# Selective scan with a mixture of experts on one core: turned state, scaled copies and sums cut into halves of the chunk

## What is computed

```
x_one = ln(x);  u = ln(x_one)*g1 + b1
x_in, z = split(u @ in_w.T);  xc = silu(causal_conv4(x_in))          # 256 channels
dt, B, C = split(xc @ xproj_w.T);  delta = softplus(dt @ dt_w.T + b)
h[t,d,n] = exp(delta[t,d]*A[d,n]) * h[t-1,d,n] + delta[t,d]*xc[t,d]*B[t,n]   # 16 states n
y[t,d]   = sum_n h[t,d,n] * C[t,n] + xc[t,d]*D[d]
x_two = x_one + (y * silu(z)) @ out_w.T
x = x + x_two + silu(gate)*val @ ffp_w.T + ffp_b      # gate, val from ln(x_two)
out = x + sum over the top 2 of 8 experts of w_e * (silu(m@Wg_e)*(m@Wu_e)) @ Wd_e    # m = ln(x)
```

## Time and profile before

| | |
|---|---|
| median of 3 runs | 898.7 us (896.98 to 903.21) |
| the profiled execution | 898.42 us, span 896.5 us |
| mean granted TensorE clock | 0.884 |
| busy: PE / DVE | 666.5 us (74%) / 726.3 us (81%) |
| busy: ACT / POOL | 504.6 us (56%) / 573.2 us (64%) |

### The profile page before, as it was taken

The page is one execution under the profiler, slowest core; times in us unless marked ns, Lnnn a source line. Parts: engine busy times, 40 slices in busy tenths (PEclk is TensorE's granted clock), DMA queues, the critical chain, the costliest instruction groups (busy, mean ns, idle before and its releaser), DMA issues. The chain is left out here.

```text
span 896.5 us, 13066 instructions
## 1 busy us (share of the span) xinstructions
PE 666.5 (74%) x3706; PEld 481.6 (54%) x3706; DVE 726.3 (81%) x1128; ACT 504.6 (56%) x1092; POOL 573.2 (64%) x488
## 2 busy tenths in 40 slices
PE   4358578678768886797788768877884877898963
PEld 2134245445335534774477446744673556798963
DVE  1378779989998999979998999999999865474363
ACT  2547676766766576556756575557553663443421
POOL 1095556566856895789768985888669934345332
PEclk9679699889879977998799988988797889999997
DMA  6833133213312336542654255434642423457794
GB/s 179 248 113 114 47 94 118 79 65 108 119 48 90 106 100 185 152 127 86 186 162 118 90 171 155 125 106 132 173 150 80 129 63 99 135 160 216 204 311 130
DMA packets 95450, 118.24 MB, mean 132 GB/s; under 512 B 11351, under 2 KB 63395, under 8 KB 95363
## 3 DMA queue, kind: packets, MB, share of 16 engines
q1 hardware_dynamic: 90835, 108.02, 41.3%
q0 software_dynamic: 4544, 9.38, 2.9%
HBM read 105.37 MB, written 16.34 MB: 136 GB/s over the span
## 5 line engine op out<-in xcount | busy, mean ns | idle before, releaser
L695 POOL TENSOR_TENSOR inflow<-du,b_wide 128x1024 f32<-128x1024 f32 x128 | 316.2, 2473 | 170.6 <-DVE product L960 109.4
L950 DVE TENSOR_TENSOR_SCAN state<-decay,carry,inflow 128x512 f32<-128x512 f32 x192 | 235.0, 1265 | 6.2 <-ACT decay L814 5.8
L814 ACT ACTIVATE decay<-delta,a_neg 128x512 f32<-128x512 f32 x256 | 171.9, 690 | 104.6 <-DVE state L950 101.1
L722 POOL DMA_INDIRECT y_dram<-y_rows,x_rows x78 | 86.8, 1112 | 82.0 <-ACT y_rows L870 73.4
L960 DVE TENSOR_TENSOR product<-state,c_wide 128x1024 f32<-128x1024 f32 (+1 forms) x98 | 135.8, 1386 | 2.8 <-PE y L1150 1.7
L1150 PE MATMUL y<-ident,product 128*128 128x128 f32 x704 | 106.2, 297 | 41.9 <-DVE product L960 41.8
L1150 PEld LDWEIGHTS y<-ident,product 128*128 128x128 f32 x704 | 87.2, 153 | 79.9 <-DVE product L960 50.0
L1155 PE MATMUL y<-h_rows,ident 128*128 128x512 f32 x160 | 101.2, 755 | 33.6 <-ACT h_rows L779 33.6
L716 POOL DMA_INDIRECT row_dram<-m_tok,place x64 | 72.7, 1136 | 25.8 <-issue 19.8
L950 DVE TENSOR_TENSOR_SCAN state<-decay,inflow 128x512 f32<-128x512 f32 x64 | 74.8, 1212 | 9.2 <-ACT decay L814 6.6
L1106 PE MATMUL work_front<-u_t,w_tap 128*128 128x512 f32 x128 | 64.1, 628 | 6.0 <-ACT u_t L750 4.4
(11 more groups left out here) (210 smaller groups left out, 1285.1 us busy)
## 6 DMA issues: line engine op xcount, KB each, us to landing
b_wide<-bc_dram SPq DMA_DIRECT2D x128, 256.0 KB, 3.3
w_stage<-gate_up_dram SPq DMA_DIRECT2D x78, 344.0 KB
c_wide<-bc_dram SPq DMA_DIRECT2D x98, 256.0 KB, 3.5
x_rows<-row_dram SPq DMA_DIRECT2D x78, 65.0 KB, 3.6
x_tok<-in_x SPq DMA_DIRECT2D x8, 256.0 KB, 6.2
out<-x_tok SPq DMA_DIRECT2D x8, 256.0 KB, 4.6
inflow<-y_dram SPq DMA_DIRECT2D x6, 256.0 KB, 4.2
gate_up_dram<-in_Wg SPq DMA_DIRECT2D x1, 1376.0 KB, 8.9
```

What stands on the lines that cost most here:

```text
L695: e.tensor_tensor(inflow[:, key % 3], du[:, c % 2], b_wide[:, key % ROW_SLOTS:key % ROW_SLOTS + 1, :].to_broadcast([P, HALVES, CHUNK]), AL ...
L722: e.indirect_dma_start(y_dram, bass.IndirectOffsetOnAxis(x_rows[:, key % X_SLOTS, ID_AT:ROW].bitcast(u32), 0), y_rows[:, key % Y_SLOTS, :] ...
L814: e.activation(decay_bank[h][:], delta[:, c % 2, h, :], ACT.Exp, scale=a_neg[:, h, n:n + 1]).then_inc(S["decay"], 1)
L950: e.tensor_tensor_scan(state[:, key % STATE_SLOTS, h, :], decay_bank[h][:], inflow[:, key % 3, h, :], 0.0 if c % (SEQ // CHUNK) == 0 else ...
```

## The change

`total`, `h_turn` and `c_scale` are each cut into two steps, one for each half of the chunk (each half is one bank of `y_bank` and one of `h_bank`). The semaphores `y_sum` and `h_turn` count halves, and each step waits for its own half alone: `h_turn0` for the first two copies of the unit before, `c_scale0` for `h_turn0` and the first half's sum, each half of `y_gate` for its own sum. In `plan()` the sum over the second half of unit i-1 (`total1`) moves behind `scan` and `decay` if unit i is shared: in a full share unit the list has `h_turn0`, `c_scale0`, `total1` of the unit before, `h_turn1`, `c_scale1`; in a half share unit `total1`, `h_turn1`, `c_scale1`. The second part of a row of `BACK`, which holds `n_t` and `m_t`, `y_cols` and `gate_h`, now comes ahead of these steps; that of `FRONT` stays behind them. The sets of shared units are the same.

```
@@ plan() @@
         if i:
-            put("total", i - 1)
+            put("total0", i - 1)
+            if i not in shares:
+                put("total1", i - 1)
         put_all(back[0], front[0])
...
+        put_all(back[1])
         if i in shares:
-            put("h_turn", i)
-            put("c_scale", i)
-        put_all(back[1], front[1])
+            if share_of(c, n) == SUB:
+                put("h_turn0", i)
+                put("c_scale0", i)
+            put("total1", i - 1)
+            put("h_turn1", i)
+            put("c_scale1", i)
+        put_all(front[1])
@@ counts @@
-        turned = [sum(k > 0 for k in share[:i + 1]) for i in range(len(UNITS))]
+        turned = [sum(share[:i + 1]) // 2 for i in range(len(UNITS))]
@@ ScalarE @@
-                elif name == "c_scale":
+                elif name in ("c_scale0", "c_scale1"):
+                    r = int(name[-1])
                     c, n = UNITS[key]
-                    e.wait_ge(S["h_turn"], turned[key])
-                    e.wait_ge(S["y_sum"], key)
+                    e.wait_ge(S["h_turn"], turned[key] - 1 + r)
+                    e.wait_ge(S["y_sum"], 2 * key - 1 + r)
                     e.wait_ge(S["c_rows"], c + 1)
-                    for sub in range(SUB - share[key], SUB):
+                    for sub in (2 * r, 2 * r + 1):
@@ VectorE @@
                     if key >= 2:
-                        e.wait_ge(S["y_sum"], key - 1)
+                        e.wait_ge(S["y_sum"], 2 * (key - 1))
...
                 elif name == "y_gate":
-                    e.wait_ge(S["y_sum"], D_STATE * (key + 1))
...
                     for r in range(2):
+                        e.wait_ge(S["y_sum"], 2 * D_STATE * (key + 1) - 1 + r)
@@ TensorE @@
-                    alone = SUB - share[key]
-                    if alone:
+                    if 2 * r < SUB - share[key]:
                         e.wait_ge(S["times_c"], products[key])
-                    for s in range(alone):
-                        for h in range(HALVES):
...
+                        for s in (2 * r, 2 * r + 1):
+                            for h in range(HALVES):
...
-                    if share[key]:
-                        e.wait_ge(S["c_scaled"], scaled[key])
-                    for r in range(alone // 2, 2):
+                    else:
+                        e.wait_ge(S["c_scaled"], scaled[key] - 2 * (1 - r))
                         t = e.matmul(y_bank[r][:], ident[:], h_rows[:, 2 * r:2 * r + 2, :].rearrange("p s d -> p (s d)"), start=False, stop=n == D_STATE - 1,
...
-                elif name == "h_turn":
+                elif name in ("h_turn0", "h_turn1"):
+                    r = int(name[-1])
                     e.wait_ge(S["scan"], HALVES * (key + 1))
                     if scaled[key] > share[key]:
-                        e.wait_ge(S["c_scaled"], scaled[key] - share[key])
+                        e.wait_ge(S["c_scaled"], scaled[key] - share[key] - 2 * (1 - r))
```

More of the change, by code:

```diff
@@ L123, with share_of @@
 HELD_ROUND = CHUNKS - 3
+def share_of(c, n):
+    return (SHARES_LAST if c == CHUNKS - 1 else SHARES).get(n, 0)
 def plan(shares=()):
@@ L267, in plan @@
         send()
-        if not moving and ("x_turn", m) not in done and n in (SHARES_LAST if c == CHUNKS - 1 else SHARES):
+        if not moving and ("x_turn", m) not in done and share_of(c, n):
             free.append(i)
         put("times_c", i)
-    put("total", len(UNITS) - 1)
+    for r in range(2):
+        put(f"total{r}", len(UNITS) - 1)
     queue_back(CHUNKS - 1)
@@ L446, in mamba_moe_block @@
         pair_of = [0 if m < tail else (1, 0, 2)[(m - tail) % 3] for m in range(len(JOBS))]
-        share = [(SHARES_LAST if c == CHUNKS - 1 else SHARES)[n] if i in shares else 0 for i, (c, n) in enumerate(UNITS)]
+        share = [share_of(c, n) if i in shares else 0 for i, (c, n) in enumerate(UNITS)]
         products = [sum(k < SUB for k in share[:i + 1]) for i in range(len(UNITS))]
         scaled = [sum(share[:i + 1]) for i in range(len(UNITS))]
-        turned = [sum(k > 0 for k in share[:i + 1]) for i in range(len(UNITS))]
+        turned = [sum(share[:i + 1]) // 2 for i in range(len(UNITS))]
         c_fetched = [sum(share[j] < SUB for j in range(i % ROW_SLOTS, i + 1, ROW_SLOTS)) for i in range(len(UNITS))]
         place_of = {step: k for k, step in enumerate(order)}
-        tiles_ahead = {i: sum(place_of["y_rows", m] < place_of["h_turn", i] for m in range(len(JOBS))) for i in shares}
-        scaled_ahead = [max((scaled[i] for i in shares if place_of["c_scale", i] < place_of["x_turn", m]), default=0) for m in range(len(JOBS))]
+        tiles_ahead = {i: sum(place_of["y_rows", m] < place_of["h_turn1", i] for m in range(len(JOBS))) for i in shares}
+        scaled_ahead = [max((scaled[i] for i in shares if place_of["c_scale1", i] < place_of["x_turn", m]), default=0) for m in range(len(JOBS))]
         held_by = [max((q for q in range(m) if pair_of[q] == pair_of[m]), default=None) for m in range(len(JOBS))]
@@ L1132, in _ @@
                     t.then_inc(S["z"], 1)
-                elif name == "total":
+                elif name in ("total0", "total1"):
+                    r = int(name[-1])
                     c, n = UNITS[key]
-                    if n == 0:
+                    if n == 0 and r == 0:
                         e.wait_ge(S["xc"], c + 1)
@@ L1144, in _ @@
                         t.then_inc(S["y_skip"], 1)
-                    alone = SUB - share[key]
-                    if alone:
+                    if 2 * r < SUB - share[key]:
                         e.wait_ge(S["times_c"], products[key])
-                    for s in range(alone):
-                        for h in range(HALVES):
-                            t = e.matmul(y_bank[s // 2][:, y_at(s, h)], product[:, key % 2, h, s * P:(s + 1) * P], ident[:],
-                                         is_transpose=True, start=False, stop=n == D_STATE - 1, skip_group_check=True)
-                    if share[key]:
-                        e.wait_ge(S["c_scaled"], scaled[key])
-                    for r in range(alone // 2, 2):
+                        for s in (2 * r, 2 * r + 1):
+                            for h in range(HALVES):
+                                t = e.matmul(y_bank[r][:, y_at(s, h)], product[:, key % 2, h, s * P:(s + 1) * P], ident[:],
+                                             is_transpose=True, start=False, stop=n == D_STATE - 1, skip_group_check=True)
+                    else:
+                        e.wait_ge(S["c_scaled"], scaled[key] - 2 * (1 - r))
                         t = e.matmul(y_bank[r][:], ident[:], h_rows[:, 2 * r:2 * r + 2, :].rearrange("p s d -> p (s d)"), start=False, stop=n == D_STATE - 1,
@@ L1162, in _ @@
                     t.then_inc(S["c_turn"], 1)
-                elif name == "h_turn":
+                elif name in ("h_turn0", "h_turn1"):
+                    r = int(name[-1])
                     e.wait_ge(S["scan"], HALVES * (key + 1))
                     if scaled[key] > share[key]:
-                        e.wait_ge(S["c_scaled"], scaled[key] - share[key])
+                        e.wait_ge(S["c_scaled"], scaled[key] - share[key] - 2 * (1 - r))
                     if tiles_ahead[key]:
                         e.wait_ge(S["y_rows"], tiles_ahead[key])
-                    for s in range(SUB - share[key], SUB):
+                    for s in (2 * r, 2 * r + 1):
                         for h in range(HALVES):
-                            t = e.transpose(h_bank[s // 2][:, y_at(s, h)], state[:, key % STATE_SLOTS, h, s * P:(s + 1) * P], ident[:])
+                            t = e.transpose(h_bank[r][:, y_at(s, h)], state[:, key % STATE_SLOTS, h, s * P:(s + 1) * P], ident[:])
                     t.then_inc(S["h_turn"], 1)
```

## The result

The changed kernel takes 876.4 us (median of 4 runs, 875.53 to 878.53) against 898.1 us for the kernel before in the same comparison (4 runs, 896.98 to 903.21). The ratio is 0.9758 with a 95% interval of 0.9729 to 0.9786. The forecast was 881.4, range 873 to 891. The profiled execution took 878.53 us with a span of 876.8, which is 19.7 less than before; the mean granted clock is 0.884, as before.

A forecast was written before the change was run, and what follows sets the result against it. DVE sets the pace of the scan, so only its idle time can be gained. Savings of 4.7 + 3.6 + 1.6 + 8.3 = 18.2 us, less 1.2 for the clock, give 17.0: 898.4 to 881.4 us, range 873 to 891.

The forecast's parts named there:

- Chunks 3 to 6: In these chunks the only full unit stands alone and DVE is dense, so nothing would be saved.
- Chunk 0: At its end DVE's three waits, 6.4 us in all, would shrink to 1.7, saving 4.7 us.
- Chunk 1: Router's wait shrinks by 3.0 us, y_gate's 1.0 goes, less 0.2 on ACT and some rounding: 3.6 us saved.
- at the unit before the router that costs ACT 0.2: The second copies start behind sum 1 of the unit before; m_tok and decay queue behind them, costing 0.2 us.
- Chunk 2: Router's wait falls from 1.90 to 0.5 us, top's 0.4 goes, less 0.2: 1.6 us saved.
- Chunk 7: Waits for decay, router, top, rank and y_gate shrink by 1.5, 2.1, 1.75, 0.9 and 2.3 us: 8.3 saved.
- Clock: 1.2 us taken off the saving for PE's lower clock level; bounds were 9 us lost or 4 gained.
- rival B: Slower: PE only at 1.2 GHz where full units follow closely, 5.1 us a unit against 4.52; 909 us, chance 0.05.
- Rival C: Nothing: gaps close but DVE meets another bound, or the tail takes the gain back; 896 us, chance 0.07.
- Rival A: Half the gain: sum 1 before turn 1 delays second copies at low clock, decay follows late; 889 us, chance 0.13.
- rival D: More: the clock stays up and ACT's table-load stretches shrink too, 25 us saved; 873 us, chance 0.12.
- The collisions: DVE instructions stalling beside POOL's inflow: plus or minus 2.5 us each, a few of them, taken as zero.

The follow-up runs named there:

- repeated pair: The kernel before and the changed kernel run again, without any edit, on another chip: 901.1 and 885.28 us, ratio 0.978.
- Experiment 3: The changed kernel, but both halves of the sum of the unit before stand together at the head of every unit: 884.97 us, ratio 0.9801.
- third comparison: The changed kernel, unedited, timed once more against the kernel before, apart from the earlier chips: 881.05 us, ratio 0.9721.
- kernel with late units: The changed kernel, but the second sum is postponed only in units n 13 to 15: 881.46 us, ratio 0.9744; timed again 881.22, ratio 0.9714.

## Why the prediction was right

The mechanism came about: the loop's steps overlap, the period fell from 4.52 to 3.46, and the waits named shrank. That the total fits as well as it does (17.0 predicted, 19.7 in the profiled pair) is in part luck. The four ends, for which 18.2 were predicted, gave 14.3 us, and 13.9 in the repeated pair. Chunks 3 to 6, for which nothing was predicted, gave 5.3 and 5.7.

**Chunk 0 (4.7 predicted, 4.7 measured).** The match is in part luck. The loop's period was 3.46 and not 3.7, and none of the rest that I kept at the second silu and at `y_gate` stayed; with the product's wait of 1.7 us, which I hadn't counted, the idle time fell by 7.7. The busy time rose by 3.0 (product on 128x1024 by 1.7 over 7 instructions, `shift` by 1.6), which I had taken as zero. The decay wait that I put at 0.8 behind `y_gate` is instead at 110.43, with 0.84.

**Chunk 1 (3.6 predicted, 0.4 measured) is the term that was wrong**, and the step that failed is "at the unit before the router that costs ACT 0.2". The router's wait of 3.36 did go. But look at ACT ahead of it (sum and turn on PE, copies and decay on ACT, then DVE's scan; `m_tok`, 1.64 us at 182.73, is left out):

```profile
179.31 1.92 PE L1168 MATMUL y<-h_rows,ident 128*128 128x512 f32 x2
...
181.02 0.95 PE L1185 MATMUL up<-ident,state 128*128 128x128 f32 x4
...
182.00 0.84 ACT L793 ACTIVATE h_rows<-up,c_tok 128x256 f32<-128x256 f32 x2 [1.61 <-PE up L1185]
...
184.27 1.29 ACT L828 ACTIVATE decay<-delta,a_neg 128x512 f32<-128x512 f32 x2
...
185.08 2.46 DVE L964 TENSOR_TENSOR_SCAN state<-decay,carry,inflow 128x512 f32<-128x512 f32 x2 [2.06 <-ACT decay L828]
...
187.65 0.19 DVE L1013 TENSOR_TENSOR logits<-work_side,b_route 128x32 f32<-128x32 f32 x1
```

The second pair of copies (182.00) waited 1.61 us for the up bank's turn (181.02), and that stood behind the sum over the second half of the unit before (179.31), which took 1.92 us. `m_tok` and decay queue behind the copies, and the scan waits 2.06 us, where it waited 0.3 before. The step's mechanism was named, but not its price: 1.7 us and not 0.2, for I had reckoned one sum at full clock, in part hidden, and in this stretch the granted clock is 0.57 (178 to 182 us). It comes again in the other two traces of the changed kernel: sums of 1.91 and 1.92 us, a granted clock of 0.57, waits of 2.08 and 2.11. Experiment 3 shows the cause by undoing it: with the sum ahead the wait is 0.46, though the granted clock is 0.59 there too (182 to 186). A second loss, at the start of the chunk, was not in any step: 1.36 for the product and 1.12 for `x_two`; the first came with the low clock at 127 us and was absent in the repeated run, the second (0.94 to 1.12) came in four traces with this order, against 0.17 before, and so goes with the order. In the repeated pair chunk 1 gained 2.0 us (80.2 to 78.2), so the term is 0.4 to 2.0.

**Chunk 2 (1.6 predicted).** Idle time fell by 1.8: router 1.90 and top 0.40 gone, 0.9 less at a decay wait, 1.6 more at the one before the router (1.90 at 266.39, the same cause as above).

**Chunk 7 (8.3 predicted, 6.2 measured).** DVE's waits there after, to be held against those of the earlier trace rows:

```profile
713.80 0.19 DVE L1013 TENSOR_TENSOR logits<-work_side,b_route 128x32 f32<-128x32 f32 x1 [2.07 <-PE work_side L1231]
...
719.43 0.17 DVE L1040 TENSOR_SCALAR top_w<-top_w 128x4 f32<-128x4 f32 x1 [1.26 <-ACT top_w L869]
...
726.40 0.69 DVE L982 TENSOR_TENSOR y_gated<-silu_z,y 128x512 f32<-128x512 f32 x1 [2.67 <-PE y L1168]
```

Here the waits did what was said, in sum: 15.7 us of them before and 7.0 after, 8.6 less. Single ones were off. The router's stayed at 2.07, since PE ran at 0.58 from 710 to 719; in the third comparison, with 0.84 in that window, the same kernel waited 0.67 there and the chunk took 74.5 us. To make up for it two waits of the feed-forward (1.39 and 0.69 before, 2.1 together) went, which I hadn't listed, and `y_gate` fell by 2.8 instead of 2.3 (its second half then waits 0.41 more, behind the cut). What kept 2.4 us of it back is busy time of DVE. The two small instructions by which I had bounded such collisions cost, before,

```profile
L886 DVE SCALAR_TENSOR_TENSOR shift<-mean_var,rstd 128x4 f32<-128x4 f32 x2 | 2.9, 1461 | 0.0
```

and after

```profile
L900 DVE SCALAR_TENSOR_TENSOR shift<-mean_var,rstd 128x4 f32<-128x4 f32 x2 | 5.0, 2482 | 0.0
```

2.1 us more for the same two instructions.

**Chunks 3 to 6 (nothing predicted, 5.3 measured).** Idle time there is unchanged within 0.2 us (15.7 and 15.9), as predicted. The gain in this pair is busy time: the same collisions, in the other direction. It is no accident of one execution: three traces of the changed kernel have 364.3 to 364.5 us here, two of the kernel before 369.6 and 370.0 (in that second pair 3.9 of the 5.7 are busy time and 1.9 idle). So "nothing" was wrong for this term, by a quarter of the whole gain, and which edit brings it is not shown: neither the halves alone nor the move alone has it (372.6 and 369.3). In chunk 3 a residual addition on 128x512 ran, before, as

```profile
334.66 4.68 POOL L695 TENSOR_TENSOR inflow<-du,b_wide 128x1024 f32<-128x1024 f32 x2
...
337.30 2.58 DVE L989 TENSOR_TENSOR x_tok<-x_two,x_tok 128x512 f32<-128x512 f32 x1
```

and after as

```profile
325.49 5.13 POOL L708 TENSOR_TENSOR inflow<-du,b_wide 128x1024 f32<-128x1024 f32 x2
...
327.50 0.90 DVE L1003 TENSOR_TENSOR x_tok<-x_two,x_tok 128x512 f32<-128x512 f32 x1
```

Two inflows of POOL follow one another in both. Before, the addition began 0.3 us after the second one (each takes 2.34) and ended half a microsecond behind it; after, it began 0.3 before the first one ended, came in between the two, and POOL's pair took 0.45 more. That is 1.7 of the 2.9 us by which DVE's busy time fell in this chunk; 1.1 more is one product on 128x512, 2.76 to 1.63. The addition took 2.58 and 2.87 in the two traces before, and 0.90, 0.90 and 0.91 in the three of the changed kernel. The Trainium skill (SBUF — State Buffer, "SBUF: two separate sides") says that GpSimd and a VectorE instruction with two inputs in SBUF share a pair of ports, which whoever starts first holds for its whole instruction, while the other blocks. By that rule the addition runs only when the inflow it met is over, and the trace agrees: it ends 0.54 us after it in the kernel before and 0.57 after it in the other, where the second inflow then was the one held up. That is read from rows; I made no run that moves one instruction alone.

**Clock (1.2 taken off).** The mean granted clock is 0.884 in both, so rival B had no ground: the chunks with many full units show 0.84, 0.91, 0.88, 0.84 before and 0.78, 0.91, 0.90, 0.80 after. In this pair it fell a little in chunks 0 and 7, and did not collapse. Rival C fell with the tail, which is 150.4 against 150.5; in the repeated pair it took back 1.2 us (155.6 against 154.4). Rival A's mechanism is real: the late decay before the router of chunks 1 and 2 is what it describes. But its price was 1.7 and 1.6 us in two places, not 9. The result lies between the forecast and rival D, though neither by a clock that stayed up nor by shorter table loads.

In sum: 18.2 us of idle time were predicted and 19.4 measured; by chunk 4.7 and 7.7, 3.6 and 1.3, 1.6 and 1.8, 0 and -0.1, 8.3 and 8.6. The collisions, taken as zero with 2.5 us for each, summed to -0.3 in this pair of traces, out of parts of +3.0, +0.9, -1.2, -2.9, -1.5, -0.3, -0.8, +2.4 and +0.1. In the repeated pair the span fell by 18.5 us, with 7.1 in chunk 0 and 2.8 in chunk 7.

## What to carry to other kernels

Where a loop over several engines runs its steps one after another, count the loads of each engine: here, cutting the buffer in two, with a count for each half, brought the period down to about the largest load, and the place of the second sum did not matter for it. An evacuation that somebody waits for belongs ahead of the bulk work of its engine; look what then comes late behind it. Measure a gain of 2 us against the spread that clock and collisions make between executions of one kernel before building on it, and read a stretch as idle plus busy time, since the two can move against each other. Look at the stretches that the change doesn't aim at, too: here they held a quarter of the gain.

## What the runs showed of the hardware that was not expected

The granted clock at a given place is not a property of the kernel alone. Two executions of the changed kernel show 0.76 and 1.00 in 127 to 134 us, and two of the kernel with late units show 1.00 and 0.50 at the end of chunk 1, where PE had been idle for 0.95 us in the one and 2.06 in the other. Elsewhere it comes back: in the 4 us in which the two halves of the turn stand in chunk 1 (178 to 182 us in the first trace), three traces of the changed kernel all show 0.57.

An instruction of VectorE on 128x4 (`shift`) took 0.13 us alone and up to 2.77 beside an inflow of POOL, and one on 128x512 (the residual addition) took 0.69 to 2.88, depending on how much of the inflow was still to run. Who started first doesn't decide it alone: the `shift` of 2.77 us began at 410.92 in the kernel before, 0.39 us ahead of the inflow that it ended with, while POOL had an indirect DMA in issue.
